# Self-attention: a head's rounded and remaining values of v in one weight load, and the last tiles' outputs in another order

## The chip, the cores and the metric

The kernel runs on one core of a Trainium2 chip. The metric is the device time of one execution in microseconds (us). Before the change its median is 3544.89 us over three runs, from 3540.25 to 3545.07.

## What is computed

A residual cross-attention of 4096 tokens (2 sequences of 2048, width 512) over a short context, and then a stack of two layers, each a windowed self-attention and a gated feed-forward block. The change lies in the self-attention, with 8 heads of 64 and a window of 256:

```
h = shift_token(x); q, k, v = split(h @ wqkv)
q = l2norm(q) * qs;  k = l2norm(k) * ksc;  q, k = rotary_xpos(q, k)
sim = where(mask, -max, (8 q) . k)      # own window of 256 and the one before
o = softmax(sim) @ v
x = x + o @ wo
```

All of it is in float32. TensorE's fast format (`F32R`) holds a rounded value, so the kernel splits an operand in two: a rounded part, `_h` (high), and what is left of it, `_l` (low). A product of two split operands is the sum of three: high by high, high by low, low by high.

## The kernel before

`attention_phase` runs once per layer. It goes through `NT` = 32 tiles of 128 tokens. Each engine has its own list of work in a fixed order, written out by hand; semaphores tie the lists together. A cycle of the loop over `t` mixes work of several tiles:

- **TensorE** (from line 1237): `turn_and_weigh(t, 0)`; `transpose_qk(t+1, 1)`; the projections of q and k for tile t+2 (`project`), with the scores of tile t+1's first four heads between them; `turn_and_weigh(t, 1)`; `output(t-1)`; the scores of the other four heads; `transpose_qk(t+2, 0)`; the projection of v, `project(t+2, 2)`; `transpose_h(t+3)`.
- **ScalarE** writes the rounded parts (`hi_v`, `hi_h`, `hi_p`, `hi_qk`, `hi_o`), the squares for the norms, the exponentials, and scales P by the reciprocals (`divide`).
- **VectorE** writes the remainders (`lo_v`, `lo_h`, `lo_p`, `lo_qk`, `lo_o`), reduces and applies the norms of q and k, adds the mask to the scores (`masked`), takes the reciprocals (`recip`) and adds the residual (`residual`, L1618).
- **POOL** takes the roots of the norms and rotates q and k. SyncE issues the loads and stores.

`turn_and_weigh` (L1328) turns P of four heads, so that keys lie on the partitions: 4 heads by 3 key blocks. Between the transposes it multiplies the P of four other heads, turned half a tile before, by v. `weigh` (L1312) loads v_h of one head and key block (128 keys by 64) and streams 256 columns past it, the rounded P and its remainder; `weigh_rest` (L1319) loads v_l and streams the 128 columns of the rounded P. Both add up in `O_BANK` and the bank after it, on partitions 0 to 63. `lo_o` (L1599) takes the results of four heads: for even and odd heads, (result of the rounded P) minus its rounded value, into `o_rest`, and then plus (result of the remainder of P), into `oT[1]`. These are 4 instructions of 64x256 in each half tile. Each `lo_o` frees the results' banks: the first `weigh` of the next half waits for its count `dv_o` (L1354).

Two banks, 0 and 1, are taken in turn by the transposed h, the projections, the transposed q and k and the output (`turn`, L1067). So `project(t+2, 2)` waits (L1263) for the residual add of tile t-1, which stands on VectorE behind `lo_o(t, 0)` (L1675).

At the end of the phase VectorE also takes the moments of the feed-forward block's first 512 rows (after tile NT-2's list, L1686) and normalises them in the last tile's list (L1655), before its reciprocals. TensorE ends with `turn_and_weigh(NT, 0)`, which only weighs, and the last outputs.

Of the kernel before, what the change touches and what calls it, by code (L numbers as in the profile page):

```python
# [1000 lines left out]
def attention_phase(nc, io, ps, ident, s, neg_half, l, h_in, y_in, w, dram, ahead):  # L1001
# [3 lines left out]
    with ExitStack() as st:  # L1005
# [9 lines left out]
        v = [sb(f"v_{x}", [P, V_SLOTS, D], F32R) for x in "hl"]  # L1015
# [64 lines left out]
        def bank_y(t):  # L1080
            return turn(7 * t + 10)
# [9 lines left out]
        def results(odd, part):  # L1091


            return ps[0:DH, O_BANK:O_BANK + 2, :].rearrange("p c (o x t) -> p c o x t", o=2, x=2)[:, :, odd, part, :]

        with nc.Block() as block:
# [140 lines left out]
            def _(e):  # L1237
# [13 lines left out]
                def project(t, a):  # L1251
# [3 lines left out]

                    if t == 1 and a:
# [55 lines left out]
                def weigh(t, h, k):  # L1312

                    n = HEADS * t + h
                    out = ps[0:DH, O_BANK + h % LANES // 2, h % 2 * 2 * P:(h % 2 + 1) * 2 * P].rearrange("p (x t) -> p x t", x=2)
                    e.matmul(out, v[0][:, (t - 2 + k) % V_SLOTS, h * DH:(h + 1) * DH], pT[:, n % 4, :, k * P:(k + 1) * P],  # L1316
                             start=k == first_block(t), stop=False)

                def weigh_rest(t, h, k):  # L1319

                    n = HEADS * t + h
                    last = e.matmul(ps[0:DH, O_BANK + h % LANES // 2, h % 2 * 2 * P:h % 2 * 2 * P + P],  # L1322
                                    v[1][:, (t - 2 + k) % V_SLOTS, h * DH:(h + 1) * DH], pT[:, n % 4, 0, k * P:(k + 1) * P],
                                    start=False, stop=k == 2)
# [3 lines left out]
                def turn_and_weigh(t, half):  # L1328
# [3 lines left out]
                    behind = None  # L1332
                    for h in range(LANES * half, LANES * half + LANES):
# [6 lines left out]
                        for k in range(3):  # L1340
# [4 lines left out]
                            if tv >= 0 and k >= first_block(tv):  # L1345
                                if behind is not None:
                                    weigh_rest(*behind)
# [8 lines left out]
                                behind = (tv, hv, k)  # L1356
                    if behind is not None:
                        weigh_rest(*behind)

                def output(t, c0, c1):  # L1360
                    if t < 0:
                        return
                    if c0 == 0:
# [767 lines left out]
```

## Time and profile before

| | |
|---|---|
| median of three runs | 3544.89 us |
| the profiled execution | 3546.84 us, its span 3545.0 us |
| granted TensorE clock, mean | 0.988 |
| self-attention of layer 1, 2 | about 600 to 1310 us, 2085 to 2795 us |

A row of the timeline has the start in us from the span's start, the length in us, engine, line, operation, what is written <- what is read (for a product: moving operand, then weights), and in brackets how long the engine was idle before and who ended that. PE is TensorE's product, PEld its weight load, DVE VectorE, ACT ScalarE. Products overlap in the records, so their pace is read from start to start.

### The profile page before, as it was taken

How to read it: one execution, taken by the hardware profiler on the slowest of the kernel's cores; microseconds unless marked ns; L12 is line 12 of the kernel's file. 1: busy time of each engine (PE TensorE's matmuls, PEld its weight loads, DVE VectorE, ACT ScalarE, POOL GpSimd, SP SyncE). 2: the span in 40 equal slices, each digit the busy share in tenths (PEclk: the TensorE clock that was granted, in tenths of full speed). 3: DMA queues.
4: the chain of work that ended last, by engine and by line, in shares of the span. 5: the costliest groups of instructions: out<-in, count | busy, mean ns of one | idle time of the engine just before them, and what ended most of it. 6: DMA issues, size and time to landing. Idle time of an engine off the chain costs nothing. (4 is left out here: it accounts for less than half of the span.)

```text
span 3545.0 us, 53886 instructions
## 1 busy us (share of the span) xinstructions
PE 3398.0 (96%) x19120; PEld 2774.8 (78%) x19120; DVE 2081.1 (59%) x4743; ACT 1782.7 (50%) x4490; POOL 1132.4 (32%) x1011
## 2 busy tenths in 40 slices
PE   6999998999999989999999979999999899999999
PEld 5666676888888867888888868888888678888887
DVE  6888876888788864222332258887888543333332
ACT  5666664777777763111111148777777521111111
POOL 3433434555555510000000045555555021110111
PEclk9999999999999999999999989999999999999999
DMA  4112203111111122011111111111111421111111
GB/s 124 43 46 65 72 35 133 49 61 60 61 60 61 61 92 95 28 43 44 44 43 44 65 66 61 61 61 60 61 60 58 128 93 50 43 39 50 49 34 37
DMA packets 186909, 216.10 MB, mean 61 GB/s; under 512 B 27142, under 2 KB 125702, under 8 KB 186643
## 3 DMA queue, kind: packets, MB, share of 16 engines
q1 hardware_dynamic: 186643, 212.65, 18.4%
q8 instruction: 155, 2.54, 0.3%
q14 instruction: 111, 0.91, 0.1%
HBM read 125.79 MB, written 69.00 MB: 55 GB/s over the span
## 5 line engine op out<-in xcount | busy, mean ns | idle before, releaser
L2042 DVE SCALAR_TENSOR_TENSOR u_full<-banks,b_cols,gate 128x512 f32<-128x512 f32 (+1 forms) x176 | 132.1, 751 | 873.2 <-ACT gate L2001 871.4
L2001 ACT ACTIVATE gate<-banks,b_cols 128x512 f32<-128x512 f32 (+1 forms) x176 | 121.2, 689 | 1018.5 <-PE banks L48 1018.5
L46 PE MATMUL banks<-fxT_h,w_h 128*128 128x512 f32 (+1 forms) x1408 | 556.8, 395 | 2.5 <-DVE w_l L2027 2.3
L48 PE MATMUL banks<-fxT_h,w_l 128*128 128x512 f32 (+1 forms) x1408 | 556.8, 395 | 0.0
L47 PE MATMUL banks<-fxT_l,w_h 128*128 128x512 f32 (+1 forms) x1408 | 555.9, 395 | 0.0
L1316 PE MATMUL banks<-pT,v_h 128*64 128x256 f32 x1440 | 412.5, 289 | 3.5 <-DVE oT_l L1610 3.5
L1342 PE MATMUL banks<-ident,prob 128*128 128x128 f32 x1440 | 382.4, 274 | 22.9 <-ACT prob L1467 17.8
L1322 PE MATMUL banks<-pT,v_l 128*64 128x128 f32 x1440 | 399.7, 294 | 0.0
L1896 POOL TENSOR_TENSOR sums<-sums,b_rows 128x512 f32<-128x512 f32 x64 | 84.9, 1358 | 887.3 <-DMA sums<-z_rows 887.3
L1196 POOL TENSOR_TENSOR rn<-ssq,neg_half 128x8 f32<-128x8 f32 x128 | 210.9, 1647 | 409.0 <-DVE ssq L1554 408.1
L46 PE MATMUL banks<-wqkv_h,hT_h 128*128 128x512 f32 x768 | 322.4, 420 | 7.3 <-DVE hT_l L1546 7.1
L1596 DVE TENSOR_TENSOR pT<-banks,pT 128x384 fp32r<-128x384 f32 (+2 forms) x512 | 268.1, 531 | 103.6 <-ACT pT L1473 97.1
L1473 ACT ACTIVATE pT<-banks 128x384 fp32r<-128x384 f32 (+2 forms) x512 | 239.9, 471 | 165.2 <-PE banks L1322 162.2
L46 PEld LDWEIGHTS banks<-fxT_h,w_h 128*128 128x128 f32 (+1 forms) x1408 | 260.2, 185 | 70.0 <-DVE w_l L2027 3.6
L48 PEld LDWEIGHTS banks<-fxT_h,w_l 128*128 128x128 f32 (+1 forms) x1408 | 260.8, 185 | 67.4
L47 PEld LDWEIGHTS banks<-fxT_l,w_h 128*128 128x128 f32 (+1 forms) x1408 | 260.5, 185 | 67.1
L48 PE MATMUL banks<-wqkv_h,hT_l 128*128 128x512 f32 x768 | 305.2, 397 | 0.0
L47 PE MATMUL banks<-wqkv_l,hT_h 128*128 128x512 f32 x768 | 304.8, 397 | 0.0
L1458 ACT ACTIVATE prob<-neg_s,neg_m 128x384 f32<-128x384 f32 (+2 forms) x512 | 299.7, 588 | 3.1
L1467 ACT ACTIVATE prob<-prob,rc 128x384 f32<-128x384 f32 (+2 forms) x512 | 269.0, 585 | 46.2 <-DVE rc L1591 46.1
L46 PE MATMUL banks<-w_h,u_h 128*128 128x512 f32 x640 | 251.8, 393 | 0.5 <-DVE u_l L2047 0.5
L47 PE MATMUL banks<-w_l,u_h 128*128 128x512 f32 x640 | 250.6, 392 | 0.0
(191 smaller groups left out, 7896.4 us busy)
## 6 DMA issues: line engine op xcount, KB each, us to landing
y_rows<-sums SPq DMA_DIRECT2D x16, 1024.0 KB
sums<-y_rows SPq DMA_DIRECT2D x64, 256.0 KB, 2.9
z_rows<-sums SPq DMA_DIRECT2D x64, 256.0 KB, 2.0
sums<-z_rows SPq DMA_DIRECT2D x16, 1024.0 KB, 5.7
thirds<-in_w SPq DMA_DIRECT2D x30, 512.0 KB, 4.9
thirds<-in_x SPq DMA_DIRECT2D x8, 1024.0 KB, 6.7
thirds<-y_rows SPq DMA_DIRECT2D x64, 128.0 KB, 2.7
thirds<-y_late SPq DMA_DIRECT2D x64, 128.0 KB, 3.2
```

Source lines behind the costliest of these rows:

```text
L46: pe.matmul(out, a_h, b_h, start=start, stop=False)
L47: pe.matmul(out, a_h, b_l, start=False, stop=False)
L48: return pe.matmul(out, a_l, b_h, start=False, stop=stop)
L1196: e.tensor_tensor(rn[:, a, :], ssq[:, a, :], neg_half[:, 0:HEADS], ALU.pow).then_inc(s["pl_rn"], 1)
L1316: e.matmul(out, v[0][:, (t - 2 + k) % V_SLOTS, h * DH:(h + 1) * DH], pT[:, n % 4, :, k * P:(k + 1) * P], start=k == first_block(t), stop=F ...
L1322: last = e.matmul(ps[0:DH, O_BANK + h % LANES // 2, h % 2 * 2 * P:h % 2 * 2 * P + P], v[1][:, (t - 2 + k) % V_SLOTS, h * DH:(h + 1) * DH], ...
L1342: last = e.transpose(ps[:, bank_head(h), k * P:(k + 1) * P], prob[:, n % 4, k * P:(k + 1) * P], ident[:])
L1458: e.activation(prob[:, m, seen(t)], neg_s[:, m, seen(t)], ACT.Exp, bias=neg_m[:, m:m + 1], scale=-1.0, accum_out=sm[:, m:m + 1]).then_inc( ...
L1467: e.activation(prob[:, m, seen(t)], prob[:, m, seen(t)], ACT.Copy, scale=rc[:, m:m + 1]).then_inc(s["ac_p"], 1)
L1473: e.activation(pT[:, n % 4, 0, seen(t)], ps[:, bank_head(h), seen(t)], ACT.Copy).then_inc(s["ac_t"], 1)
L1596: e.tensor_tensor(pT[:, n % 4, 1, seen(t)], ps[:, bank_head(h), seen(t)], pT[:, n % 4, 0, seen(t)].bitcast(F32), ALU.subtract).then_inc(s[ ...
L2042: e.scalar_tensor_tensor(out=u_full[r, m % 2, :], in0=ps[r, 2 * (m % 2), :], scalar=b1[r, place[m], 0:1], in1=gate[r, :], op0=ALU.add, op1 ...
```

## The change

v becomes one tensor in which a head's rounded values and their remainder stand side by side: 128 columns, one weight load. One product of 256 columns then gives, on partitions 0 to 63, rounded v by both parts of P, and on 64 to 127 the remainder of v by both parts of P; `weigh_rest` is gone (1440 products). `lo_o` now adds three shares: rounded by rounded minus its rounded value, plus rounded v by the remainder of P, plus the remainder of v by rounded P. So each half tile has 6 instructions instead of 4. The share of both remainders is computed and not used. `hi_v` and `lo_v` write with a stride.

In the last tiles the order changes. TensorE projects v of tile 31 directly after `turn_and_weigh(29, 1)`. The output of tile 28 moves behind the transposes of k of tile 31; tile 29's output is cut in two halves, one after `turn_and_weigh(30, 1)`, one before `turn_and_weigh(31, 1)`; its bank and its waits change. VectorE adds the residuals of 28 and 29 later, and in tile 31 takes both reciprocals right after `lo_p`, ahead of `lo_o(30, 1)` and the normalisation. ScalarE scales the first pair of heads before the last two exponentials, and rounds tile 30's second half after all scalings.

```diff
-        v = [sb(f"v_{x}", [P, V_SLOTS, D], F32R) for x in "hl"]
+        v = sb("v", [P, V_SLOTS, HEADS, 2, DH], F32R)
...
-            return turn(7 * t + 10)
+            return turn(7 * t + 10) if t < NT - 4 else t % 2
...
-        def results(odd, part):
-            return ps[0:DH, O_BANK:O_BANK + 2, :].rearrange("p c (o x t) -> p c o x t", o=2, x=2)[:, :, odd, part, :]
+        def results(odd, rest_v=0, rest_p=0):
+            rows = slice(DH * rest_v, DH * rest_v + DH)
+            return ps[rows, O_BANK:O_BANK + 2, :].rearrange("p c (o x t) -> p c o x t", o=2, x=2)[:, :, odd, rest_p, :]
...
+                    elif a == 2 and t == NT - 1:
+                        e.wait_ge(s["dv_norm"], nth(2 * NT, 2 * t + 1))
                     elif a == 2 and t:
                         e.wait_ge(s["dv_y"], nth(NT, t - 2))
...
-                def weigh_rest(t, h, k):
...
+                    out = ps[:, O_BANK + h % LANES // 2, h % 2 * 2 * P:(h % 2 + 1) * 2 * P].rearrange("p (x t) -> p x t", x=2)
+                    last = e.matmul(out, v[:, (t - 2 + k) % V_SLOTS, h].rearrange("p x d -> p (x d)"),
+                                    pT[:, n % 4, :, k * P:(k + 1) * P], start=k == first_block(t), stop=k == 2)
...
-                        e.wait_ge(s["dv_norm"], nth(2 * NT, min(2 * t + 7, 2 * NT)))
-                        if t >= NT - 3:
-                            e.wait_ge(s["dv_r"], nth(2 * NT, 2 * NT))
-                        if t == NT - 1:
+                        if t < NT - 4:
+                            e.wait_ge(s["dv_norm"], nth(2 * NT, 2 * t + 7))
+                        elif t < NT - 2:
+                            e.wait_ge(s["dv_r"], nth(2 * NT, 2 * NT - 1 + t % 2))
+                        else:
                             e.wait_ge(s["dv_y"], nth(NT, t - 1))
...
                         project(t + 2, 0)
+                        if t == NT - 2:
+                            output(t - 2, 0, DC)
                         scores(t + 1, 0)
                         project(t + 2, 1)
+                        if t == NT - 1:
+                            output(t - 2, DC // 2, DC)
                     turn_and_weigh(t, 1)
-                    output(t - 1, 0, DC // 2)
+                    if t < NT - 3:
+                        output(t - 1, 0, DC)
+                    elif t == NT - 3:
+                        project(NT - 1, 2)
+                    else:
+                        output(t - 1, 0, DC // 2)
                     if t == NT - 1:
                         turn_and_weigh(NT, 0)
-                    output(t - 1, DC // 2, DC)
+                        output(t - 1, DC // 2, DC)
                     scores(t + 1, 1)
                     transpose_qk(t + 2, 0)
-                    project(t + 2, 2)
+                    if t < NT - 3:
+                        project(t + 2, 2)
...
# ScalarE
-                    hi_o(t - 1, 1)
+                    if t < NT - 1:
+                        hi_o(t - 1, 1)
                     exponent(t, 4)
                     exponent(t, 5)
                     squares(t + 2, 0)
+                    if t == NT - 1:
+                        divide(t, 2)
                     exponent(t, 6)
                     exponent(t, 7)
-                    divide(t, 2)
+                    if t < NT - 1:
+                        divide(t, 2)
                     divide(t, 3)
+                    if t == NT - 1:
+                        hi_o(t - 1, 1)
...
# VectorE: lo_o
                     for odd in range(2):
-                        e.wait_ge(s["dv_or"], nth(4 * NT, 4 * t + 2 * half + odd + 1))
+                        e.wait_ge(s["dv_or"], nth(8 * NT, at_half + odd + 1))
                         r = slice(DH * odd, DH * odd + DH)
-                        ins = e.tensor_tensor(oT[1][r, t % 2, 2 * half:2 * half + 2, :], results(odd, 1), o_rest[r], ALU.add)
+                        e.tensor_tensor(o_rest[r], results(odd, rest_p=1), o_rest[r], ALU.add).then_inc(s["dv_or"], 1)
+                    for odd in range(2):
+                        e.wait_ge(s["dv_or"], nth(8 * NT, at_half + odd + 3))
+                        r = slice(DH * odd, DH * odd + DH)
+                        ins = e.tensor_tensor(oT[1][r, t % 2, 2 * half:2 * half + 2, :], results(odd, rest_v=1), o_rest[r], ALU.add)
...
# VectorE: the order
-                    lo_o(t - 1, 1)
+                    if t < NT - 1:
+                        lo_o(t - 1, 1)
+                    recip(t, 2)
                     if t == NT - 1:
+                        recip(t, 3)
+                        lo_o(t - 1, 1)
+                        residual(t - 2)
                         ffn_normalise(e, ahead["s"], ahead["t"], l, 0)
-                    recip(t, 2)
...
                     lo_o(t, 0)
-                    residual(t - 1)
+                    if t == NT - 2:
+                        residual(t - 2)
+                    elif t != NT - 3:
+                        residual(t - 1)
```

## Rows read from the trace of the kernel before

**Rows 1.** The page: busy time of each engine, with its share of the span.
```profile
PE 3398.0 (96%) x19120; PEld 2774.8 (78%) x19120; DVE 2081.1 (59%) x4743; ACT 1782.7 (50%) x4490; POOL 1132.4 (32%) x1011
```
**Rows 2.** One cycle by windows: PE, PEld, DVE, ACT, POOL, clock, DMA share, GB/s.
```profile
847.32:869.45 22.13, 22.13 (x158) 19.00 (x157) 18.00 (x50) 17.66 (x42) 11.95 (x12) 1.00 0.16 49
```
**Rows 3.** TensorE's waits from 850 to 1230 us: total, times, longest.
```profile
PE banks L1287 <- POOL m L1213: 2.2, 2, 1.4
```
**Rows 4.** Timeline of VectorE: four of the residual adds of layer 1.
```profile
669.62 0.69 DVE L1618 TENSOR_TENSOR sums<-banks,sums 128x512 f32<-128x512 f32 x1
...
935.14 0.69 DVE L1618 TENSOR_TENSOR sums<-banks,sums 128x512 f32<-128x512 f32 x1
...
1017.75 0.69 DVE L1618 TENSOR_TENSOR sums<-banks,sums 128x512 f32<-128x512 f32 x1
...
1239.03 0.69 DVE L1618 TENSOR_TENSOR sums<-banks,sums 128x512 f32<-128x512 f32 x1
```
**Rows 5.** Timeline of TensorE: a turn's first product, the one after it, the next turn, projection.
```profile
850.84 0.27 PE L1342 MATMUL banks<-ident,prob 128*128 128x128 f32 x1
...
854.30 0.60 PE L1287 MATMUL banks<-ident,m 128*128 128x128 f32 x4
...
861.70 0.27 PE L1342 MATMUL banks<-ident,prob 128*128 128x128 f32 x1
...
869.70 0.48 PE L46 MATMUL banks<-wqkv_h,hT_h 128*128 128x512 f32 x1
```
**Rows 6.** Timeline of TensorE in layer 2's last weighing, without transposes.
```profile
2785.30 0.28 PE L1316 MATMUL banks<-pT,v_h 128*64 128x256 f32 x1
2785.42 0.22 PE L1322 MATMUL banks<-pT,v_l 128*64 128x128 f32 x1
...
2785.65 0.28 PE L1316 MATMUL banks<-pT,v_h 128*64 128x256 f32 x1
```
**Rows 7.** Groups of weight loads by line: busy us, mean ns of one, idle.
```profile
L1316 PEld LDWEIGHTS banks<-pT,v_h 128*64 128x64 f32 x1440 | 196.3, 136 | 9.8 <-issue 4.3
...
L1306 PEld LDWEIGHTS banks<-kT_l,qT_h 64*128 64x128 f32 x512 | 50.7, 187 | 0.0
```
**Rows 8.** Timeline of TensorE: scores with 256 columns, two row halves at once.
```profile
966.99 0.28 PE L1306 MATMUL banks<-kT_l,qT_h 64*128 64x256 f32 x2
...
967.46 0.28 PE L1306 MATMUL banks<-kT_h,qT_l 64*128 64x256 f32 x2
```
**Rows 9.** Timeline of VectorE in one cycle.
```profile
851.24 0.69 DVE L1567 TENSOR_TENSOR v_l<-banks,v_h 128x512 fp32r<-128x512 f32 x1 [1.28 <-ACT v_h L1438]
...
856.23 0.87 DVE L1605 TENSOR_TENSOR o_rest<-banks,oT_h 64x256 f32<-64x256 f32 x2
857.13 0.85 DVE L1610 TENSOR_TENSOR oT_l<-banks,o_rest 64x256 fp32r<-64x256 f32 x2
...
862.53 0.69 DVE L1552 TENSOR_REDUCE ssq<-sq 128x8 f32<-128x512 f32 x1 [0.70 <-ACT sq L1432]
...
866.39 0.68 DVE L1560 TENSOR_TENSOR qk<-banks,rn 128x512 f32<-128x512 f32 x1
...
868.76 0.69 DVE L1618 TENSOR_TENSOR sums<-banks,sums 128x512 f32<-128x512 f32 x1
```
**Rows 10.** Timeline of ScalarE in the same cycle.
```profile
859.39 2.12 ACT L1467 ACTIVATE prob<-prob,rc 128x384 f32<-128x384 f32 x4
861.89 0.60 ACT L1432 ACTIVATE sq<-banks 128x512 f32<-128x512 f32 x1 [0.39 <-PE banks L48]
```
**Rows 11.** Timeline of POOL in the same cycle.
```profile
863.50 1.64 POOL L1196 TENSOR_TENSOR rn<-ssq,neg_half 128x8 f32<-128x8 f32 x1 [0.25 <-DVE ssq L1554]
```
**Rows 12.** Timeline of VectorE: the last residual add of layer 1.
```profile
1309.43 0.69 DVE L1618 TENSOR_TENSOR sums<-banks,sums 128x512 f32<-128x512 f32 x1 [3.09 <-PE banks L48]
```
**Rows 13.** Timeline of TensorE: tile 31's second half begins.
```profile
1292.04 0.47 PE L1342 MATMUL banks<-ident,prob 128*128 128x128 f32 x1 [6.80 <-ACT prob L1467]
```
**Rows 14.** The stretch behind that hole by windows, columns as in rows 2.
```profile
1292.00:1294.97 2.97, 2.93 (x16) 2.94 (x17) 0.24 (x1) 1.99 (x4) 0.00 (x0) 0.50 0.02 6
```

More of the change, by code:

```diff
@@ L1314, in weigh @@
                     n = HEADS * t + h
-                    out = ps[0:DH, O_BANK + h % LANES // 2, h % 2 * 2 * P:(h % 2 + 1) * 2 * P].rearrange("p (x t) -> p x t", x=2)
-                    e.matmul(out, v[0][:, (t - 2 + k) % V_SLOTS, h * DH:(h + 1) * DH], pT[:, n % 4, :, k * P:(k + 1) * P],
-                             start=k == first_block(t), stop=False)
-                def weigh_rest(t, h, k):
[L1321 to L1324, printed above, removed]
+                    out = ps[:, O_BANK + h % LANES // 2, h % 2 * 2 * P:(h % 2 + 1) * 2 * P].rearrange("p (x t) -> p x t", x=2)
+                    last = e.matmul(out, v[:, (t - 2 + k) % V_SLOTS, h].rearrange("p x d -> p (x d)"),
+                                    pT[:, n % 4, :, k * P:(k + 1) * P], start=k == first_block(t), stop=k == 2)
                     if k == 2:
@@ L1331, in turn_and_weigh @@
                     tv, half_v = (t, 0) if half else (t - 1, 1)
-                    behind = None
                     for h in range(LANES * half, LANES * half + LANES):
@@ L1345, in turn_and_weigh @@
                             if tv >= 0 and k >= first_block(tv):
-                                if behind is not None:
-                                    weigh_rest(*behind)
                                 if k == first_block(tv):
@@ L1355, in turn_and_weigh @@
                                 weigh(tv, hv, k)
-                                behind = (tv, hv, k)
-                    if behind is not None:
-                        weigh_rest(*behind)
                 def output(t, c0, c1):
@@ L1481, in hi_o @@
                     for odd in range(2):
-                        e.activation(oT[0][DH * odd:DH * odd + DH, t % 2, 2 * half:2 * half + 2, :], results(odd, 0), ACT.Copy
+                        e.activation(oT[0][DH * odd:DH * odd + DH, t % 2, 2 * half:2 * half + 2, :], results(odd), ACT.Copy
                                      ).then_inc(s["ac_o"], 1)
@@ L1566, in lo_v @@
                         e.wait_ge(s["ac_v"], nth(NT, t + 1))
-                        e.tensor_tensor(v[1][:, t % V_SLOTS, :], ps[:, bank_qkv(t, 2), :], v[0][:, t % V_SLOTS, :].bitcast(F32),
+                        e.tensor_tensor(v[:, t % V_SLOTS, :, 1, :], token_major_heads(ps[:, bank_qkv(t, 2), :]),
+                                        v[:, t % V_SLOTS, :, 0, :].bitcast(F32),
                                         ALU.subtract).then_inc(s["dv_v"], 1)
@@ L1602, in lo_o @@
                     e.wait_ge(s["ac_o"], nth(4 * NT, 4 * t + 2 * half + 2))
+                    at_half = 4 * (2 * t + half)
                     for odd in range(2):
                         r = slice(DH * odd, DH * odd + DH)
-                        e.tensor_tensor(o_rest[r], results(odd, 0), oT[0][r, t % 2, 2 * half:2 * half + 2, :].bitcast(F32),
+                        e.tensor_tensor(o_rest[r], results(odd), oT[0][r, t % 2, 2 * half:2 * half + 2, :].bitcast(F32),
                                         ALU.subtract).then_inc(s["dv_or"], 1)
                     for odd in range(2):
-                        e.wait_ge(s["dv_or"], nth(4 * NT, 4 * t + 2 * half + odd + 1))
+                        e.wait_ge(s["dv_or"], nth(8 * NT, at_half + odd + 1))
                         r = slice(DH * odd, DH * odd + DH)
-                        ins = e.tensor_tensor(oT[1][r, t % 2, 2 * half:2 * half + 2, :], results(odd, 1), o_rest[r], ALU.add)
+                        e.tensor_tensor(o_rest[r], results(odd, rest_p=1), o_rest[r], ALU.add).then_inc(s["dv_or"], 1)
[3 more added lines that the diff above has]
+                        ins = e.tensor_tensor(oT[1][r, t % 2, 2 * half:2 * half + 2, :], results(odd, rest_v=1), o_rest[r], ALU.add)
                     ins.then_inc(s["dv_o"], 1)
@@ L1663, in _ @@
                     masked(t + 1, 1)
-                    if t:
+                    if 0 < t < NT - 1:
                         recip(t, 3)
```

2 lines of the change are left out of this document (1 added, 1 removed).

## The prediction

> **What bounds the kernel now.** The page's busy line comes first: TensorE is busy 96% of the span and VectorE 59% [rows 1], but that mixes phases. One cycle of self-attention (one tile of 128 tokens) lasts 22.13 us, with TensorE recorded busy throughout, VectorE for 18.00 and ScalarE for 17.66 [rows 2]. Between 850 and 1230 us TensorE waited for VectorE or ScalarE not once, and 2.2 us for POOL [rows 3]. So TensorE sets the cycle, and VectorE has only 4.1 us to spare. I count cycles by the add of the residual: from 669.62 to 935.14 us are 12 of 22.13 us, from 1017.75 to 1239.03 us 10 more, and between them 4 shorter ones, 82.61 us together, where the second sequence begins with few key blocks [rows 4]. The second layer runs the same program, so 44 full cycles count.
>
> **TensorE's part.** A full cycle has 24 triples of a transpose, a 256-column product with v_h and a 128-column product with v_l. Twelve triples take 854.30 - 850.84 = 3.46 us, 0.288 each [rows 5]. Where no transposes are left, v_h takes 0.12 and v_l 0.06 from start to start, 0.175 for both (two such pairs from 2785.30 to 2785.65) [rows 6]; the transpose is the remaining 0.114. The change drops v_l's product, and v_h's weights become 128 columns wide instead of 64. The new pair has no row. From below: nothing but v_l goes, 0.288 - 0.057 = 0.231 (v_l at 0.057, the same 128 columns that v_h's 256 have twice). From above: the wider load isn't hidden at all and the saving is gone, 0.288 or more, as a recorded load takes 136 ns at 64 columns and 187 ns at 128 [rows 7]. The nearest row has 128-column loads under 256-column products, and four steps from 966.99 to 967.46 give 0.117 each [rows 8]; the transpose, at 0.114, is about as long a cover. I take 0.117 + 0.117 = 0.234. That saves 0.054 x 24 = 1.3 us a cycle: TensorE alone would need 20.83 us.
>
> By the Trainium skill (TensorE: Matmul & The Clock Gate, "LDWEIGHTS" and "Back-to-back issue gap") a load takes its columns over 1.2 ns, so the load doubles to 107 ns, and a warm product its columns over 2.4 plus 2.5 ns. The triple would be 0.22 by that; rows 5 have 0.288, so the trace disagrees for the transpose. The new pair would be bound by its two loads, some 0.216, and the forecast some 9 us lower.
>
> **VectorE's part.** Each half tile has two subtractions of 64x256 (0.87 us from 856.23) and two adds (0.85 from 857.13) [rows 9]. The change puts two more adds between, priced as the existing pair of adds with the wait behind it, 0.88 (0.85 and some 0.03): 1.76 us a cycle. The strided writes of v keep their 512 elements; I cost them at nothing, bounded by 0 and the 0.1 by which such an instruction's length differs between rows. VectorE then works 19.8 us, and its order matters: TensorE's projection of v for tile t+2 waits for the residual add of tile t-1. That ended at 868.76 + 0.69 = 869.45, and the projection began at 869.70 [rows 5, 9]: 0.25 us of slack, against four added adds in a cycle, two of them just in front of it. So a loop closes: residual, projection of v, rounding on ScalarE, then VectorE's whole list up to the next residual. I lay it out from the residual's end (R = 847.32 us before, one cycle below 869.45):
>
> - v_l begins at R + 3.92 now (851.24). The projection can follow R by 0.1 instead of 0.25: R + 3.77.
> - The first four remainders of P are paced by TensorE, a head of three triples being 3 x 0.288 = 0.86. With three pairs, 0.70, they save 0.16 twice and some 0.13 at the last: 0.45. Then the added adds, +0.88.
> - The reduction for k's norms begins at R + 15.21 after 0.70 us idle (862.53). VectorE's busy list before it would be done at 14.51 - 0.15 - 0.45 + 0.88, less 0.1 for a shorter wait at q's squares: R + 14.7 at the latest. The squares themselves: k's projection ends on TensorE where the next turn begins, 861.70 or R + 14.38 now, 0.65 + 0.15 sooner then, R + 13.6 [rows 5]; ScalarE's squares follow 0.19 later and take 0.60, unless its four scalings of P (2.12, two behind a reciprocal of VectorE that comes 0.2 later) still run [rows 10]. That gives about 14.6. I take R + 14.65.
> - The next four remainders go at TensorE's pace: the turn begins 0.8 sooner and their last is ready 0.6 sooner in it. k's normalisation, at R + 19.07 now (866.39), comes at 19.07 - 0.8 - 0.6 = R + 17.67. POOL's root for it could start 0.25 before 863.50 and takes 1.64 [rows 11]: ready at about R + 17.5, so hardly any slack is left there.
> - From there to the residual's end is 3.06 us now; with the added adds 3.94.
>
> R to R is 21.6 us. TensorE then stands for 0.8 us a cycle at the projection of v, a wait that isn't there today. Gain: 0.53 x 22 = 11.7 us a layer.
>
> **The rest of a layer.** In the four short cycles TensorE has few pairs to save and VectorE still pays 1.76: between 0 and +7 us, I take +2.5. The fill at the phase's start: 0 to +1.8, I take +1. The last tiles: now 70.4 us pass from the residual add of tile 27 (ends 1239.72) to that of tile 31 (ends 1309.43 + 0.69) [rows 4, 12], with a hole of 6.80 us on TensorE before the second half of tile 31 and 2.97 us at half clock behind it (granted 0.50, that is 1.2 GHz) [rows 13, 14]. VectorE was then behind the feed-forward layer's moments and normalisation. The change takes the projection of tile 31's v out of the residual's wait, which starts tile 30 some 3 us sooner, and moves the reciprocals ahead. But in tile 31 the first product with v needs the results' banks, so VectorE's six instructions on tile 30's second half. ScalarE's rounding for them now stands behind the last exponentials and scalings, after a second reciprocal that itself waits for those. Laid out in the same way, this second half begins 53 us after the residual of tile 27 (52 now), the hole comes back as 9 us, and the last residual ends at 70.9: +0.5. The other bounds are -4, if what replaces the hole is short enough to keep the clock, and +5, if the clock falls twice. The outputs moved (12 or 6 products each, same count) cost nothing: they fill waits. The moved bank of these outputs removes waits on normalisations long done.
>
> **Sum.** A layer: -11.7 + 2.5 + 1 + 0.5 = -7.7; two layers -15. The profiled execution took 3546.84 us (span 3545.0), 2 above the runs' median of 3544.89. It would be 3531.5, and the median **3530 us**.
>
> **Rivals.**
> - *VectorE's loop sets it (forecast), chance 0.58.* 3517 to 3542, for a cycle of 21.4 to 21.8. For: 0.25 us of slack and 0.88 added. Measurement tells about 0.2%, 7 us, from no change: 0.50 of this is faster, 0.08 the same.
> - *TensorE still sets the cycle, 0.12.* If VectorE's added work fits its 4.1 us idle, the cycle is 20.83: 44 x 1.3 = 57 less, 8 back for the rest: 3496. Against it stands the residual's place at the end of its list.
> - *It cancels, 0.15.* A pair at about 0.25 lets TensorE arrive 0.4 later at each turn, the cycle is 22.0 to 22.1, and the time 3545 to 3550.
> - *Slower, 0.15.* The 128-column load doesn't hide behind the transpose. It decides from a pair of 0.253 on, where the loop is at 22.13; above, each 0.01 costs 0.24 us a cycle. At 0.288 TensorE saves nothing, the loop absorbs the 0.70 idle and 0.15 of slack, and the cycle is 22.13 + 1.76 - 0.85 = 23.04: 44 x 0.91 + 8 = +48, 3593 us. Rows 8 speak against it, with loads of half height; no row has a load of full height under so short a cover.
> - That the change doesn't do what it says (the drop of 1440 products) I hold for impossible by the diff; that the last tiles lose instead is in their bounds.
>
> Faster 0.62, same 0.23, slower 0.15. The range is 3490 to 3562: it takes in TensorE's bound, the cancelling case and the slower one up to a pair of about 0.26; the rest of the slower one and a little below remain outside.
>
> **What would show it.** Right: starts of the new products 0.23 apart with a transpose in between; cycles of 21.6; a wait of some 0.8 us on TensorE at the projection of v with the residual add as its releaser; VectorE's idle before k's norms gone; six instructions of 64x256 a half tile in 2.65 us. Wrong: cycles of 20.8 with no such wait, pairs of 0.25 or more, or last tiles that differ from 70 us by more than 5.

## The result, and the profile after

The changed kernel takes **3556.27 us** in the median (3552.01 to 3558.93, 9 runs) against 3545.07 for the kernel before, measured beside it: a ratio of **1.0031 (95%: 1.0021 to 1.0042)**. It is slower by 11 us where 15 less were forecast. The profiled execution took 3555.66 us, with a span of 3552.8, so 7.8 over the span before.

First the busy line of the page after, as in [rows 1], and then, in the second fence, three lines of the list of waits over the whole span: who waited for whom, us in total, times, the longest.

```profile
PE 3346.0 (94%) x17680; PEld 2703.2 (76%) x17680; DVE 2180.0 (61%) x4999; ACT 1778.2 (50%) x4490; POOL 1131.5 (32%) x1011
```
```profile
PE banks L46 <- DVE sums L1634: 35.2, 56, 0.7
...
PE banks L1321 <- DVE oT_l L1626: 17.0, 4, 6.0
...
DVE f_stats L1763 <- DMA thirds<-z_late: 10.7, 3, 5.2
```

TensorE has 52 us less work and VectorE 99 more. In return TensorE now stands 56 times before the projection of v, 35.2 us in all, waiting for the residual add: the wait that was forecast. The waits of the two lines below it were not.

**The full cycles are as forecast.** VectorE's residual adds in the timeline, the same four as in [rows 4], two neighbours in the steady part, and the last one:

```profile
669.57 0.69 DVE L1634 TENSOR_TENSOR sums<-banks,sums 128x512 f32<-128x512 f32 x1
...
842.80 0.69 DVE L1634 TENSOR_TENSOR sums<-banks,sums 128x512 f32<-128x512 f32 x1
...
864.47 0.69 DVE L1634 TENSOR_TENSOR sums<-banks,sums 128x512 f32<-128x512 f32 x1
...
929.39 0.69 DVE L1634 TENSOR_TENSOR sums<-banks,sums 128x512 f32<-128x512 f32 x1
...
1014.54 0.69 DVE L1634 TENSOR_TENSOR sums<-banks,sums 128x512 f32<-128x512 f32 x1
...
1231.58 0.69 DVE L1634 TENSOR_TENSOR sums<-banks,sums 128x512 f32<-128x512 f32 x1
...
1310.82 0.69 DVE L1634 TENSOR_TENSOR sums<-banks,sums 128x512 f32<-128x512 f32 x1 [5.58 <-PE banks L48]
```

From 669.57 to 929.39 twelve cycles take 21.65 us each, and the ten from 1014.54 to 1231.58 take 21.70 in the mean (two of them 21.9). On TensorE's timeline the new pairs, as in [rows 5], and the projection of v that ends the cycle:

```profile
847.16 0.27 PE L1339 MATMUL banks<-ident,prob 128*128 128x128 f32 x1
847.18 0.37 PE L1321 MATMUL banks<-pT,v 128*128 128x256 f32 x1
847.39 0.27 PE L1339 MATMUL banks<-ident,prob 128*128 128x128 f32 x1
...
865.31 0.47 PE L46 MATMUL banks<-wqkv_h,hT_h 128*128 128x512 f32 x1 [0.64 <-DVE sums L1634]
```

A pair is 0.23 us from start to start, and TensorE stands 0.64 us at the projection. The same cycle on VectorE, as in [rows 9]:

```profile
847.32 0.69 DVE L1576 TENSOR_TENSOR v<-banks,v 128x512 fp32r<-128x512 f32 x1 [1.19 <-ACT v L1441]
...
858.11 0.69 DVE L1561 TENSOR_REDUCE ssq<-sq 128x8 f32<-128x512 f32 x1
...
861.20 0.68 DVE L1569 TENSOR_TENSOR qk<-banks,rn 128x512 f32<-128x512 f32 x1
861.80 0.85 DVE L1617 TENSOR_TENSOR o_rest<-banks,oT_h 64x256 f32<-64x256 f32 x2
862.68 0.87 DVE L1622 TENSOR_TENSOR o_rest<-banks,o_rest 64x256 f32<-64x256 f32 x2
863.58 0.87 DVE L1626 TENSOR_TENSOR oT_l<-banks,o_rest 64x256 fp32r<-64x256 f32 x2
```

The three pairs of 64x256 stand in front of the residual and end 2.65 us after the first starts. The idle time before k's norms [rows 9] is gone.

**The last tiles are not as forecast.** From the residual add of tile 27 to that of tile 31 the kernel before took 70.40 us [rows 4, 12]; after it is 1310.82 - 1231.58 = **79.24** in layer 1, and 81.43 in layer 2 (2720.66 to 2802.09). Follow the queue of SyncE around tile 28's store. SyncE's timeline after (start, duration of the issue):

```profile
1270.96 0.32 SPq L1124 DMA_DIRECT2D z_rows<-sums  x1
...
1272.29 0.45 SPq L1748 DMA_DIRECT2D thirds<-z_rows  x1
1272.78 0.51 SPq L1749 DMA_DIRECT2D thirds<-z_late  x1
```

and before:

```profile
1261.87 0.32 SPq L1122 DMA_DIRECT2D z_rows<-sums  x1
...
1263.21 0.45 SPq L1725 DMA_DIRECT2D thirds<-z_rows  x1
```

The store of tile 28 waits for that tile's residual, which the change puts one tile later (1270.24 instead of 1261.15; measured from the residual add of tile 27, 38.7 us instead of 22.1). The load of the feed-forward layer's first rows stands behind this store in SyncE's program, and so it is issued 9 us later too, though it needs nothing of tile 28. What waits for it is VectorE, and behind the moments in VectorE's list stand tile 31's reciprocals and the adds that free the results' banks:

```profile
1278.12 2.47 DVE L1763 BATCH_NORM_STATS2 f_stats<-thirds 128x6 f32<-128x512 f32 x4 [5.16 <-DMA thirds<-z_late]
...
1282.98 0.15 DVE L1601 RECIPROCAL rc<-sm 128x2 f32<-128x2 f32 x1
1285.51 0.17 DVE L1601 RECIPROCAL rc<-sm 128x2 f32<-128x2 f32 x1 [2.38 <-ACT prob L1461]
1287.53 0.86 DVE L1617 TENSOR_TENSOR o_rest<-banks,oT_h 64x256 f32<-64x256 f32 x2 [1.85 <-ACT oT_h L1485]
```

ScalarE waited 6.69 us for the first of these reciprocals, and TensorE for ScalarE's scaling. The same stretch on TensorE, with the last output (12 products from 1305.29) at its end; the third line is the last weighing, which has no transposes between its products:

```profile
1283.83 0.48 PE L1339 MATMUL banks<-ident,prob 128*128 128x128 f32 x1 [7.77 <-ACT prob L1470]
1290.33 0.55 PE L1321 MATMUL banks<-pT,v 128*128 128x256 f32 x1 [6.03 <-DVE oT_l L1626]
1298.89 1.67 PE L1321 MATMUL banks<-pT,v 128*128 128x256 f32 x12 [2.72 <-DVE oT_l L1626]
1305.29 0.80 PE L46 MATMUL banks<-wo_h,oT_h 128*128 128x512 f32 x1 [3.35 <-DVE oT_l L1626]
```

Two holes of 7.77 and 6.03 us have taken the place of the 6.80 in [rows 13]. And the windows show the last output at half clock after (columns as in [rows 2]), where before it had the full one, second fence:

```profile
1305.29:1310.70 5.41, 5.41 (x12) 3.80 (x12) 0.00 (x0) 0.00 (x0) 0.00 (x0) 0.50 0.00 0
```
```profile
1306.30:1309.40 3.10, 3.00 (x12) 2.17 (x12) 0.04 (x1) 0.00 (x0) 0.00 (x0) 1.00 0.11 37
```

**Where the 7.8 us are.** By residual adds: at tile 27 of layer 1 the kernel after is 7.45 us ahead; its last tiles give back 8.84; until the second add of layer 2 it loses 2.19 more (the first interval there is 22.75 instead of 21.51, at a granted clock of 0.92 instead of 1.00); it gains 6.85 up to tile 27 and gives back 11.06. -7.45 + 8.84 + 2.19 - 6.85 + 11.06 = +7.79. The last phase adds nothing.

### The profile page after: what moved, and what is told of

Same layout as the page of the kernel before. It is cut to its first block and busy times, and to the rows that moved or that the text cites. A ratio compares the mean times of both kernels' runs of the same rounds, so it can differ in the third digit from the quotient of the medians.

```text
span 3552.8 us, 51260 instructions
## 1 busy us (share of the span) xinstructions
PE 3346.0 (94%) x17680; PEld 2703.2 (76%) x17680; DVE 2180.0 (61%) x4999; ACT 1778.2 (50%) x4490; POOL 1131.5 (32%) x1011
## 5 line engine op out<-in xcount | busy, mean ns | idle before, releaser
L1321 PE MATMUL banks<-pT,v 128*128 128x256 f32 x1440 | 356.6, 369 | 17.0 <-DVE oT_l L1626 17.0
L1339 PE MATMUL banks<-ident,prob 128*128 128x128 f32 x1440 | 341.7, 276 | 28.4 <-ACT prob L1470 23.2
L46 PE MATMUL banks<-wqkv_h,hT_h 128*128 128x512 f32 x768 | 324.7, 423 | 42.3 <-DVE sums L1634 35.2
L1321 PEld LDWEIGHTS banks<-pT,v 128*128 128x128 f32 x1440 | 275.8, 194 | 23.6 <-issue 18.4
L1606 DVE TENSOR_TENSOR pT<-banks,pT 128x384 fp32r<-128x384 f32 (+2 forms) x512 | 250.4, 523 | 20.1 <-ACT pT L1476 5.3
```

The costliest lines, as they stand in the source:

```text
L46: pe.matmul(out, a_h, b_h, start=start, stop=False)
L1321: last = e.matmul(out, v[:, (t - 2 + k) % V_SLOTS, h].rearrange("p x d -> p (x d)"), pT[:, n % 4, :, k * P:(k + 1) * P], start=k == first_ ...
L1339: last = e.transpose(ps[:, bank_head(h), k * P:(k + 1) * P], prob[:, n % 4, k * P:(k + 1) * P], ident[:])
L1606: e.tensor_tensor(pT[:, n % 4, 1, seen(t)], ps[:, bank_head(h), seen(t)], pT[:, n % 4, 0, seen(t)].bitcast(F32), ALU.subtract).then_inc(s[ ...
```

## The experiments

There are ten further kernels. "Last tiles" is always the time from the residual add of tile 27 to that of tile 31, in layer 1 and layer 2; it is 70.4 and 70.4 before, 79.2 and 81.4 after. "Cycle" is the usual time of a full one. Ratios are to the kernel before, with 95% intervals. Each median comes from 4 to 11 runs, each span, cycle and last tiles from one profiled execution.

| kernel | median us | ratio | span | cycle | last tiles |
|---|---|---|---|---|---|
| merge_only | 3546.25 | 0.9995 (0.9986 to 1.0004) | 3542.7 | 21.65 | 75.6, 75.8 |
| tail_only | 3558.44 | 1.0032 (1.0019 to 1.0044) | 3558.2 | 22.13 | 77.7, 77.6 |
| load_first | 3543.95 | 0.9992 (0.9983 to 1.0001) | 3543.9 | 21.65 | 76.1, 74.6 |
| residual_between | 3544.22 | 0.9996 (0.9987 to 1.0005) | 3543.9 | 21.75 | 76.9, 78.3 |
| round_first | 3531.92 | 0.9961 (0.9948 to 0.9975) | 3526.8 | 21.65 | 69.6, 69.5 |
| no_third | 3473.61 | 0.9796 (0.9783 to 0.9809) | 3471.4 | 20.77 | 70.2, 68.4 |
| merge_late | 3538.84 | 0.9980 (0.9971 to 0.9988) | 3534.1 | 21.65 | 72.2, 72.3 |
| tail_cured | 3538.57 | 0.9980 (0.9970 to 0.9989) | 3535.8 | 22.13 | 67.1, 68.7 |
| round_only | 3543.16 | 0.9994 (0.9985 to 1.0003) | 3541.4 | 21.65 | 75.3, 74.9 |
| round_late | 3533.41 | 0.9967 (0.9954 to 0.9980) | 3529.3 | 21.65 | 70.6, 69.6 |

### The two halves of the change, apart

**merge_only** has one weight load and three shares, with the last tiles in the order of the kernel before; every hunk of the diff with NT - 4 to NT - 1 is undone, for instance

```
         def bank_y(t):
-            return turn(7 * t + 10) if t < NT - 4 else t % 2
+            return turn(7 * t + 10)
...
                     lo_o(t, 0)
-                    if t == NT - 2:
-                        residual(t - 2)
-                    elif t != NT - 3:
-                        residual(t - 1)
+                    residual(t - 1)
```

> The merged v with three shares, and the last tiles in the order of the kernel before. Theory (the loss lies in the reordered last tiles): cycles of 21.65 us as in the changed kernel, 72 to 73 us from the residual add of tile 27 to that of tile 31 (70.4 before, plus two longer roundings of results that nothing covers), a span of 3527 to 3532. Rival (the longer rounding of the results is what costs the last tiles 9 us): 78 us or more for the last tiles, a span of 3545 or more.

**tail_only** is the opposite: the two separate products of before, with only those hunks.

> The kernel before with the last tiles' new order alone. Theory (the residual add of tile 28, now one cycle later, holds SyncE's queue, and with it the load that VectorE's moments need): cycles of 22.13 us, the load of the feed-forward rows issued some 9 us later than before against the last tile's work, a wait of 4 us or more on VectorE before the moments, a span of 3553 to 3563. Rival (the new order by itself is a gain, and only the longer rounding spoils it): a span of 3545 or less.

tail_only is as slow as the whole change, 1.0032 against 1.0031, without any merging, and VectorE's moments wait there for the same load (timeline of VectorE, tail_only):

```profile
L1766 DVE BATCH_NORM_STATS2 f_stats<-thirds x4: 675/676/695, 1284.7 to 1286.5; 128x6 f32<-128x512 f32 x4
...
  DMA thirds<-z_late: 5.5, 1
```

(one group of instructions: shortest, median and longest ns, first and last start; below it, what its engine sat idle for). That was the theory. The new order therefore loses 7.3 us in each layer's last tiles by itself. merge_only gives the other half: its cycle is 21.65, but its last tiles lose 5.2 and 5.4 us in the old order too, with no late load. These 75.6 and 75.8 us lie between the 72 to 73 of the theory and the 78 of the rival, and the span of 3542.7 lies between theirs: neither held. The two losses don't add up: on top of the merging, the new order costs 3.6 and 5.6 us. merge_only's last tiles on TensorE, to be set beside [rows 13]:

```profile
1285.07 0.48 PE L1337 MATMUL banks<-ident,prob 128*128 128x128 f32 x1 [8.31 <-ACT prob L1457]
```

The hole is 8.31 instead of 6.80 (+1.5), the wait before the last output 3.35 instead of 2.44 (+0.9), and that output takes 5.4 us at a granted clock of 0.50 instead of 3.0 at 1.00 (+2.4): 4.8 of layer 1's 5.2. Merging alone gains nothing that can be measured: what 22 cycles bring in a layer, the short cycles, the start and the last tiles take back.

### SyncE's queue

**load_first** is the changed kernel with the load issued one tile sooner, ahead of tile 28's store.

```
-                        if i == NI - 1 and u == 2:
-
+                        if i == NI - 1 and u == 1:
                             e.wait_ge(s["pe_h"], at(NT, NI, 4, 0))
                             ffn_load_in(e, ahead["s"], ahead["t"], ahead["dram"], 0)
+                        if i == NI - 1 and u == 2:
```

> The changed kernel, but SyncE issues the load of the feed-forward rows one tile sooner, ahead of the store of tile 28. Theory: VectorE's moments begin when its list reaches them, 5.1 us sooner in each layer; the last tiles take 74 us instead of 79 and 81, and the span is 3540 to 3544. Rival (ScalarE's rounding behind the last scalings is what ends last, and takes the 5 us back): the span stays above 3549.

The time is 12.3 us below that of the changed kernel, and the span lies in the theory's range. The moments start at 1274.09 with no wait, and the first hole shrinks from 7.77 to 2.51. The second is still there (timeline of TensorE, load_first):

```profile
1279.80 0.33 PE L1339 MATMUL banks<-ident,prob 128*128 128x128 f32 x1 [2.51 <-ACT prob L1470]
1286.30 0.55 PE L1321 MATMUL banks<-pT,v 128*128 128x256 f32 x1 [6.18 <-DVE oT_l L1626]
```

Counted from the residual add of tile 27, tile 31's second half begins 5.2 us sooner in layer 1 and 4.8 in layer 2. The last residual add comes only 3.2 us sooner in layer 1 (76.1 instead of the 74 of the theory), and 6.8 in layer 2 (74.6). The difference is TensorE's clock. Between the start of that second half and the last output the stretch takes 15.0 us in the changed kernel's layer 1, at granted clocks of 0.80 and then 0.90, and 17.0 in load_first's, at 0.68 and 0.72. In layer 2 it is the other way round: 17.3 us in the changed kernel and 15.3 in load_first.

### ScalarE's order in tile 31

**round_first** is load_first with ScalarE's rounding of tile 30's second half in the place that it has in every other tile, ahead of the exponentials, and VectorE's adds for it ahead of the second reciprocal.

```
-                    if t < NT - 1:
-                        hi_o(t - 1, 1)
+                    hi_o(t - 1, 1)
                     exponent(t, 4)
...
-                    if t == NT - 1:
-                        hi_o(t - 1, 1)
...
-                        recip(t, 3)
                         lo_o(t - 1, 1)
+                        recip(t, 3)
                         residual(t - 2)
```

> The changed kernel with the early load of load_first, and in tile 31 ScalarE rounds tile 30's second half (hi_o) right after tile 31's first rounding, as in every other tile, with VectorE's adds for it before recip(31,3). load_first left TensorE waiting 6.18 us for oT_l at 1286.30, with the rounding queued behind the scalings. Theory (the order of ScalarE's list makes that hole): the wait falls to 2 us or less, the stretch from residual(27) to residual(31) goes from 76.0 and 74.6 to 72 to 73 us in each layer, the time from 3543.95 to 3537 to 3540. Rival (VectorE's list is the bound of tile 31, with six adds for each half, so that what waits first is of no weight): the 6.18 us turn into a longer wait before the weighing of 31's heads 4 to 7, the stretch stays at 74.5 to 76, the time within 0.05% of load_first.

The theory held, and by more than it said: 3531.92 us. The 6.18 us became 1.67 (timeline of TensorE, round_first):

```profile
1277.91 0.33 PE L1339 MATMUL banks<-ident,prob 128*128 128x128 f32 x1 [2.52 <-ACT prob L1470]
1279.91 0.55 PE L1321 MATMUL banks<-pT,v 128*128 128x256 f32 x1 [1.67 <-DVE oT_l L1623]
1288.32 1.69 PE L1321 MATMUL banks<-pT,v 128*128 128x256 f32 x12 [2.70 <-DVE oT_l L1623]
```

The wait before the last weighing, the rival's sign, did not grow (2.70). **round_only** has this cure without the early load.

> The changed kernel with ScalarE's rounding of tile 30's second half ahead, as in round_first, but with the next phase's rows still loaded behind the store of tile 28. With the kernel after (3556.27), load_first (3543.95) and round_first (3531.92) it closes the square of the two cures, worth 12.3 and 12.0 us in that order. Theory (the two delays lie one behind the other in VectorE's list, so each is worth its own whichever is cured first): last tiles from 79.2 and 81.4 to 73 to 75.5 us, the time 3543 to 3546, and VectorE's moments still wait about 5 us for the rows. Rival (with VectorE stopped at the moments, tile 31's first remainders are late by 5 us anyway, and the earlier rounding lies idle in front of VectorE's adds): the time falls by under 5 us, to 3551 or more.

It took 3543.16 us, the last tiles 75.3 and 74.9, and the moments still wait 5.55 us: the theory. With it all four combinations of the two cures are measured. The load is worth 12.3 us without the other cure and 11.2 with it, the rounding 13.1 and 12.0, both together 24.4. These are two delays, one behind the other in VectorE's list, each worth its own. Not all of it is waiting; a part is TensorE's clock, which differs between the four kernels. The first interval of layer 2, for one, is 22.75 us in the changed kernel and 22.74 in load_first, both at a granted clock of 0.92, and 21.17 in round_only and in round_first, both at 1.00: that is 1.6 of the rounding's 12 to 13 us.

**tail_cured** asks whether the new order would then be better than the old one without any merging: tail_only with both cures.

> The kernel before with the change's new order in the last tiles alone (as tail_only), and with both cures of it: the early load of load_first and the rounding order of round_first. Theory (the new order loses by SyncE's queue and ScalarE's list alone, 7.3 us a layer against the kernel before): last tiles 77.7 to 70 to 71.5 us, the time from 3558.4 to 3545, no different from before. Rival (moving one output and residual each to the end costs by itself, since the work that fills tile 31's holes isn't long enough): 74 us or more a layer, the time 3551 or more.

3538.57, last tiles 67.1 and 68.7: better than the theory, which had it level with the kernel before. With the two cures the new order of the last tiles is worth 7 us to that kernel; in tail_only it lost because of two steps' places, the load's and the rounding's.

### VectorE's list in the loop

**residual_between** is merge_only with the residual add ahead of the third pair of adds (except in tile 31), so that the projection of v need not wait for these.

```
                         e.tensor_tensor(o_rest[r], results(odd, rest_p=1), o_rest[r], ALU.add).then_inc(s["dv_or"], 1)
+                    if between is not None:
+                        residual(between)
                     for odd in range(2):
```

> As merge_only, and VectorE adds the residual of tile t-1 between the second and the third pair of the rounding of tile t's first half. Theory (the residual's place in VectorE's list sets the cycle): TensorE's wait of 0.64 us at the projection of v goes, the cycle is 21.0 us, the span 26 to 30 us below merge_only. Rival (VectorE's list is as long as the cycle in any order): the cycle stays at 21.4 or more, less than 12 us below merge_only.

The rival held. The wait moved and didn't go (TensorE, residual_between: one of them in the timeline, and all of them in the list of waits):

```profile
848.16 0.63 PE L1250 MATMUL banks<-ident,thirds 128*128 128x128 f32 x4 [0.78 <-DVE qT_l L1565]
```
```profile
PE banks L1250 <- DVE qT_l L1565: 40.6, 54, 0.8
```

TensorE now waits at the transposes of h for the remainder of q, the last step of VectorE's list, and the cycle is 21.75, a little longer. So it is not the residual's place that costs the cycle, but the length of the list: here the loop closes at the next of VectorE's instructions that TensorE needs.

**no_third** leaves the third share out of VectorE's sums (what is left of v times the weights is multiplied, in the same load, and not added).

```
                         e.tensor_tensor(o_rest[r], results(odd, rest_p=1), o_rest[r], ALU.add).then_inc(s["dv_or"], 1)
-                    for odd in range(2):
-                        e.wait_ge(s["dv_or"], nth(8 * NT, at_half + odd + 3))
-                        r = slice(DH * odd, DH * odd + DH)
-                        ins = e.tensor_tensor(oT[1][r, t % 2, 2 * half:2 * half + 2, :], results(odd, rest_v=1), o_rest[r], ALU.add)
```

(the add that is left then writes oT[1] itself)

> merge_only without the third share of a head's result (what is left of v times the weights) on VectorE: it is still multiplied, in the same weight load, but not added, so that part of the result is left out. That takes four adds of 0.44 us from VectorE's list of each cycle, 1.76 us, and one pair of adds from each hand-over. Theory (VectorE's added adds are what the merging costs, in the loop and in the last tiles): the cycle falls from 21.65 to TensorE's own 20.8 to 20.9 with no wait for the sums; the hole in tile 31 goes back from 8.31 to about 6.8 us, the wait before the last output from 3.35 to 2.44; with the shorter wait the last output runs at a granted clock of 1.00 and takes 2.8 us, and the last tiles take 68 to 70 us a layer; span 3485 to 3495. Rivals: in the loop another list (ScalarE's, POOL's) holds the cycle at 21.3 or more, span 3515 or more; for the clock, the last output still runs at 0.50 and takes 5.4 us, which would mean that the wait just before it is not what decides the clock.

One cycle of it by windows, columns as in [rows 2]; the cycle after is the second fence:

```profile
1160.83:1181.60 20.77, 20.77 (x135) 17.62 (x134) 17.80 (x48) 17.65 (x43) 11.95 (x12) 1.00 0.16 51
```
```profile
842.80:864.47 21.67, 21.04 (x134) 17.62 (x132) 19.61 (x51) 17.61 (x42) 11.91 (x12) 1.00 0.15 50
```

With VectorE back at 17.8 us, TensorE is busy throughout and the cycle is 20.77, close to the 20.83 that the prediction gave TensorE alone. VectorE's 1.8 us of adds therefore cost 0.88 us of each cycle. They cost more in all, 73 us of the time. Of the 71.3 between the two spans the 44 full cycles are 39.7, the last tiles 12.9, and the short cycles 12.6 (5.8 in layer 1, 85.11 against 79.35, and 6.8 in layer 2). The short cycles and some 6 us more, half of them in the first interval of each layer, were not counted when a span of 3485 to 3495 was expected. The hole in tile 31 went from 8.31 to 7.47, less than expected. And the clock's part of the expectation fell: the wait before the last output was 2.43 us as said, but its clock was not 1.00:

```profile
1267.97:1272.50 4.53, 4.52 (x12) 3.03 (x12) 0.00 (x0) 0.00 (x0) 0.00 (x0) 0.63 0.05 18
```

### The next phase's moments

**merge_late** is merge_only with the moments moved from the end of tile 30 to tile 31, ahead of its heads 4 to 7, and the scaling of these rows behind the sums of tile 31's first half. **round_late** does the like to round_first.

```
                     normalise(t + 2, 0)
+                    if t == NT - 1:
+                        ffn_moments(e, ahead["s"], ahead["t"], l, 0)
...
                     lo_o(t, 0)
+                    if t == NT - 1:
+                        ffn_normalise(e, ahead["s"], ahead["t"], l, 0)
                     residual(t - 1)
...
-                    if t == NT - 2:
-                        ffn_moments(e, ahead["s"], ahead["t"], l, 0)
```

(and `ffn_normalise`, the scaling, goes from its old place ahead of `recip(t, 2)`)

> merge_only with the moments of the next phase's first rows (2.5 us of VectorE, now at the end of tile 30) moved into tile 31 ahead of the roundings of its heads 4 to 7, and the scaling of these rows (2.2 us, now ahead of recip(31,2)) moved behind the sums of tile 31's first half. Theory (VectorE's list is what keeps the second half of tile 31 waiting in merge_only: the wait of 8.31 us before the turn of tile 31's head 4 or so follows a list longer by the moments, the scaling and the added adds): that wait falls to about 4 to 5 us, the last tiles from 75.7 to 72 to 73 us a layer, the time from 3546.25 to 3540 to 3542. Rival (the wait follows ScalarE's exponents, and VectorE's work only lies inside it; or the rows come later to the next phase, whose first turns then wait): the stretch is shorter by under 1 us or the start of the next phase later by as much, the time within 0.05% of merge_only.

> round_first with the moments of the next phase's first rows (3.0 us of VectorE with what follows them, at the end of tile 30) moved behind residual(29) in tile 31, and the scaling of these rows behind the sums of tile 31's first half. In round_first TensorE waits 2.52 us for the scaled weights of head 2 at 1277.91 and 1.67 us for oT_l at 1279.91, both behind a VectorE list that holds the moments. Theory (VectorE's list sets that stretch): the two waits fall together by 2 to 3 us, the last tiles from 69.6 to 67 us a layer, the time from 3531.9 to 3526 to 3529. Rival (what the moments give up there they take from the second half of tile 31, whose turns of heads 4 to 7 follow the same list, or the next phase's rows come late): last tiles 69 us or more, the time within 0.05% of round_first.

merge_late gained 7.4 us and 3.5 us in each layer's last tiles: there the 8.31 us hole did follow VectorE's list, and is 4.84, as the theory had it; the time is 1 us below the theory's. In round_late the rival held: it gained nothing (3533.41 against 3531.92). In layer 2 the intervals between its last residual adds equal those of round_first to 0.03 us (11.59, 11.55, 7.76 against 11.58, 11.56, 7.74). In layer 1 its last residual add follows 8.84 us behind the one before instead of 7.95, for its last output ran at a granted clock of 0.50 and that of round_first at 0.63. VectorE's timeline in layer 1 shows what became of the time that the moments no longer take:

```profile
1275.99 1.26 DVE L1603 TENSOR_TENSOR pT<-banks,pT 128x384 fp32r<-128x384 f32 x2 [0.72 <-ACT pT L1476]
1278.69 0.17 DVE L1598 RECIPROCAL rc<-sm 128x2 f32<-128x2 f32 x1 [1.44 <-ACT prob L1461]
```

It is idle there: VectorE waits for ScalarE's roundings and exponentials. With both steps in place VectorE's list doesn't set that stretch any more. round_first is the best of the versions that compute the whole result: 14 us below the kernel before, and 24 below the changed one.

## Why the prediction was wrong

**What held**, each from the end of the residual add, R = 843.49 us in the cycle shown:

| step | forecast | measured |
|---|---|---|
| pair of transpose and product | 0.234 | 0.232 (12 from 846.93 to 849.71) |
| v_l begins | R + 3.77 | R + 3.83 |
| k's norms, no idle time before | R + 14.65 | R + 14.62 |
| k's normalisation | R + 17.67 | R + 17.71 |
| from there to the residual's end | 3.94 | 3.96 |
| projection behind the residual | 0.1 | 0.15 |
| cycle | 21.6 | 21.65, two in ten 21.9 |
| TensorE's wait at the projection | 0.8 | 0.64 |
| TensorE alone | 20.83 | 20.77 (no_third) |
| short cycles of a layer | +2.5 | +2.5, +3.5 |

So the mechanism of the likeliest case was right for the full cycles, and TensorE as the bound was four adds away. By the Trainium skill (TensorE: Matmul & The Clock Gate, "LDWEIGHTS") a weight load takes its columns over 1.2 ns; an estimate from that, the two loads of a pair, is 0.213 us, where the prediction wrote some 0.216. The rows have 0.232, and the measurement decides. The rival in which the wider load isn't hidden had its deciding point at 0.253, and the pair never reached it: the kernel is slower for another reason. The measured 3556 us lies in the range of 3490 to 3562 by luck, for the upper end was set for that slower pair. None of the rivals described what made the kernel slower. Only the prediction's last sign of being wrong named the place: last tiles that differ from 70 us by more than 5.

**Small misses of size.** The full cycles gained 9.9 us in layer 1 and 10.4 in layer 2, not 11.7, since a cycle is 0.05 longer than laid out and a few are 0.3 longer. The start of layer 1 cost nothing and that of layer 2 2.2, against 1 each; 1.6 of the 2.2 come with the clock of 0.92 in its first interval (21.17 us at 1.00 in round_first). Up to tile 27 that is 7.45 and 4.66 us a layer against 8.2: 4.3 us of the miss.

**The step that failed** is the term of the last tiles, "from 70.4 to 70.9, +0.5", with bounds of -4 and +5. It measured +8.8 and +11.1, 19 of the 23 us between the forecast span (3545.0 less the 15.4 of the sum, 3529.6) and the measured 3552.8. The layout put the start of tile 31's second half 53 us after the residual of tile 27, with 9 us of holes before it. Measured: 1290.33 - 1232.27 = 58.1, with 7.77 + 6.03 = 13.8. load_first has 1286.30 - 1233.48 = 52.8, with 2.51 + 6.18 = 8.7. Up to this point the layout was thus exact for a kernel in which the load is not late, if with one hole where there are two. It had seen ScalarE's rounding behind the second reciprocal, which round_first shows to be worth another 12 us. What it left out is **SyncE's queue**: residual of tile 28, store of tile 28, load of the next phase's rows, moments. The prediction moved the residual through VectorE's, ScalarE's and TensorE's programs, and did not ask which DMA waits for it and what is issued behind that DMA. The second half of tile 31 begins 5.1 us late by this in layer 1 and 5.0 in layer 2 (58.0 instead of 53), 10.1 of the 19.

The rest is behind the start of the second half: from there to the end it takes 21.2 us in layer 1 and 23.5 in layer 2, instead of the 17.9 of the layout (18.1 before). Of these 3.3 and 5.6 us, 0.9 each is the added pair of adds in the last wait (3.35 instead of 2.44); the prediction doesn't itemise its 17.9, so whether that was in it can't be told. In each layer 2.4 are the half clock of the last output. The other 2.3 in layer 2 are half clock as well: the same turn and weighing take 17.3 us there, at 0.67 and 0.73, and 15.0 in layer 1, at 0.80 and 0.90. A clock that falls twice was in the bounds, as a risk of up to +5; it came on top of the late load and not instead of it. What sets the clock in these stretches stays open.

**The missing rival** would have been: "the moved residual delays a store, and with it what stands behind the store". It could have been read from the trace of before: the load is issued 2 us after the residual of tile 28 (1263.21 against 1261.15) with the store in between, so by this program whatever delays the one delays the other, and here the change itself put that residual a tile later.

## What to carry to other kernels

When an instruction is moved, follow its semaphore into every queue, the DMA-issuing one first: a load that has nothing to do with it may stand behind the store that waits for it. Where two lists run in lockstep, price an added operation by the list's whole length and not by its place: moving the add out of TensorE's way only moved the wait (residual_between), while taking it away gave the cycle back. And count the exceptions: 44 full cycles gave 20 us, and two layers' last four tiles gave all of it back (+19.9); with two steps in another place they took 1.6 us less than before.

## What the runs showed that had not been expected

The last output of layer 1, 12 products of 512 columns each, took different times for the same work. Before: 3.0 us at a granted clock of 1.00. In tail_only, tail_cured, no_third, round_first and round_only: 4.5 to 4.6 us at 0.62 or 0.63, which is a mix of the two levels (in round_first the first two products start 0.34 and 0.23 us apart, those from the fourth on 0.43, the last two 0.39). In merge_only, load_first, merge_late, residual_between, round_late and the changed kernel: 5.4 to 5.5 us at 0.50, that is 1.2 GHz throughout. The wait just before does not decide it: it was 2.44 before, at full clock, and 2.43 in no_third and tail_cured, at 0.63; it was 3.35 in round_first, at 0.63, and 3.35 in the changed kernel, at 0.50. Nor need the clock fall while TensorE waits: in no_third it was still at its full level when the output began, with products 0.23 us apart, and these went to 0.43 apart some 1 us later. What does decide it stays open; what it costs in layer 1, 1.5 or 2.4 us, is in every figure of the last tiles above.

At half clock a pair of transpose and product takes 0.43 us, not twice the 0.232. Two neighbouring products of merge_late's turn behind its 4.84 us hole, with a transpose between them:

```profile
1283.69 0.56 PE L1319 MATMUL banks<-pT,v 128*128 128x256 f32 x1
...
1284.12 0.56 PE L1319 MATMUL banks<-pT,v 128*128 128x256 f32 x1
```

Half of that is 0.215: some 0.017 us of the pair at full clock does not double at half. The runs don't show what it is.
